# Attention with all products of a pair of key blocks with V in one group on TensorE, and the band factors of both blocks together

## What is computed

```python
q = x @ Wq.T + bq + ocr_bias          # k, v alike; 16 heads of 32 features
scores = jnp.einsum('bhsd,bhtd->bhst', q, k) / math.sqrt(HEAD_DIM)
scores = scores + _band_mask(S, scores.dtype)     # 0.1 where |i - j| <= 2
attn = jax.nn.softmax(scores, axis=-1)
out = jnp.einsum('bhst,bhtd->bhsd', attn, v)
return out @ Wo.T + bo
```

## Time and profile before

| | us |
|---|---|
| median of three runs (lowest to highest) | 4579.53 (4577.45 to 4581.79) |
| the profiled execution, its own time | 4576.01 |
| its span in the trace | 4574.1 |
| TensorE busy in the span (97%) | 4436.7 |
| VectorE busy (74%) | 3378.5 |
| ScalarE busy (53%) | 2446.5 |
| GpSimd busy (62%) | 2828.9 |

### The profile page before, as it was taken

The page is one execution under the profiler, slowest core; times in us unless marked ns, Lnnn a source line. Parts: engine busy times, 40 slices in busy tenths (PEclk is TensorE's granted clock), DMA queues, the critical chain, the costliest instruction groups (busy, mean ns, idle before and its releaser), DMA issues. The chain is left out here.

```text
span 4574.1 us, 62800 instructions
## 1 busy us (share of the span) xinstructions
PE 4436.7 (97%) x22928; PEld 2504.6 (55%) x22928; DVE 3378.5 (74%) x5663; ACT 2446.5 (53%) x4652; POOL 2828.9 (62%) x927
## 2 busy tenths in 40 slices
PE   7999989999999999999999999999999999977999
PEld 6888845454445444444445454444454444525777
DVE  5444467888888888788787888888888788735776
ACT  2222216666666666666666666666666666651121
POOL 2111017778878787787877778878787787870000
PEclk9999969999999999999999999999999999988999
DMA  7666545555565656565656555565656565445452
GB/s 253 206 212 205 197 120 118 129 124 131 125 140 117 140 113 145 110 144 121 142 118 132 128 124 131 125 140 117 140 113 144 112 144 117 104 89 199 147 178 108
DMA packets 287700, 640.71 MB, mean 140 GB/s; under 512 B 40641, under 2 KB 107201, under 8 KB 249538
## 3 DMA queue, kind: packets, MB, share of 16 engines
q0 software_dynamic: 36864, 268.45, 29.3%
q1 hardware_dynamic: 250562, 368.66, 27.0%
HBM read 211.82 MB, written 156.24 MB: 80 GB/s over the span
## 5 line engine op out<-in xcount | busy, mean ns | idle before, releaser
L702 DVE TENSOR_REDUCE part_max<-ps_m 128x1 f32<-128x512 f32 x4096 | 2548.9, 683 | 654.0 <-PE ps_m L598 650.5
L772 POOL TENSOR_TENSOR pair<-p_sb 128x2048 f32<-128x2048 f32 x512 | 2348.4, 4587 | 665.5 <-ACT p_sb L690 301.9
L690 ACT ACTIVATE p_sb<-ps_s 128x512 f32<-128x512 f32 x4096 | 2114.8, 602 | 1130.3 <-PE ps_s L618 1129.8
L618 PE MATMUL ps_s<-q_st,k_st 97*128 97x512 f32 x4096 | 1732.4, 425 | 17.1 <-ACT p_sb L690 17.1
L598 PE MATMUL ps_m<-k_st,q_st 96*128 96x512 f32 x4096 | 1646.0, 405 | 42.0 <-POOL k_st L765 20.1
L618 PEld LDWEIGHTS ps_s<-q_st,k_st 97*128 97x128 f32 x4096 | 774.0, 189 | 1031.4 <-ACT p_sb L690 619.3
L632 PE MATMUL ps_o<-p_sb,v_sb 128*32 128x512 f32 x8192 | 1092.4, 605 | 0.2 <-DVE p_sb L729 0.2
L598 PEld LDWEIGHTS ps_m<-k_st,q_st 96*128 96x128 f32 x4096 | 785.7, 192 | 230.6 <-DVE part_max L702 76.3
L632 PEld LDWEIGHTS ps_o<-p_sb,v_sb 128*32 128x32 f32 x8192 | 161.3, 108 | 345.2 <-ACT p_sb L690 289.3
L166 POOL TENSOR_TENSOR xb<-xin,bo_row 128x2048 f32<-128x2048 f32 x16 | 75.3, 4706 | 424.7 <-DMA xin<-in_x 414.0
L642 PE MATMUL ps_d<-pair,ones 128*32 128x512 f32 x2048 | 267.5, 594 | 9.9 <-DMA pair<-pair 9.9
(11 more groups left out here) (94 smaller groups left out, 2678.4 us busy)
## 6 DMA issues: line engine op xcount, KB each, us to landing
pair<-pair POOLq DMA_DIRECT2D x256, 1024.0 KB, 7.3
q_st<-q_hi_d SPq DMA_DIRECT2D x128, 256.0 KB, 4.2
k_st<-k_hi_d SPq DMA_DIRECT2D x128, 256.0 KB, 5.5
xin<-in_x SPq DMA_DIRECT2D x16, 1024.0 KB, 8.2
xb_d<-xb SPq DMA_DIRECT2D x16, 1024.0 KB, 5.2
q_hi_d<-s_hi SPq DMA_DIRECT2D x64, 256.0 KB, 2.0
q_lo_d<-s_lo SPq DMA_DIRECT2D x64, 256.0 KB, 2.3
k_hi_d<-s_hi SPq DMA_DIRECT2D x64, 256.0 KB, 2.3
```

What stands on the lines that cost most here:

```text
L618: nc.tensor.matmul(ps_s[:, (HG * s + h) % RING_S, :], k_st[0:ROWS + 1, unit // QC % 2, kt // TT, h, kt % TT * P:(kt % TT + 1) * P], q_st[0 ...
L690: nc.scalar.activation(p_sb[:, s % SLOTS, h, :], ps_s[:, (HG * s + h) % RING_S, :], ACT.Exp, scale=SCALE).then_inc(p_ready, 1)
L702: nc.vector.tensor_reduce(part_max[:, unit % 2, col, n:n + 1], ps_m[:, seq % RING_M, :], AX.X, ALU.max).then_inc(max_taken, 1)
L772: nc.gpsimd.tensor_tensor(pair[:, m % PAIR_RING], p_sb[:, s % SLOTS], p_sb[:, (s + 1) % SLOTS], ALU.add).then_inc(paired, 1)
```

## The change

- TensorE: `weigh` of a macro's two steps and, if one is due, `add_keys` now stand together. This burst comes at odd s, after heads 0 and 1 of step s and before head 2, and has `weigh(s - 3)`, `weigh(s - 2)` and at s mod 4 = 1 `add_keys`. `add_keys` keeps its step and comes half a step earlier in it. Even steps have no product with V.
- VectorE: the two bands of macro m (steps 2m and 2m+1) stand after head 1's reduction of step 2m+2, not in front of the first one of that step.
- ScalarE: `copy_o` moves from the start of kt = 2 to the middle of kt = 1, `copy_sum` from the start of kt = 7 to the middle of kt = 5, `o_high` from the start of kt = 14 to the start of kt = 15.
- No instruction is added or removed. SyncE and GpSimd keep their programs.

```diff
--- before.py
+++ after.py
@@ -648,15 +649,20 @@
             for j in range(HG * LEAD):
                 ahead(1, j)
-            for s in range(ST + SUM_LAG - 3):
-                if s < ST:
-                    for h in range(HG):
-                        score(s, h)
-                        ahead(*max_at(s, h))
-                if 2 <= s < ST + 2:
+            def burst(s):
+                if 3 <= s < ST + 3:
+                    weigh(s - 3)
                     weigh(s - 2)
                 if s >= SUM_LAG and s % 4 == SUM_LAG % 4:
                     add_keys((s - SUM_LAG) // 4)
+
+            for s in range(ST + SUM_LAG - 3):
+                for h in range(HG):
+                    if s % 2 == 1 and h == HG // 2:
+                        burst(s)
+                    if s < ST:
+                        score(s, h)
+                        ahead(*max_at(s, h))
 
         @block.scalar
         def _(act):
@@ -676,16 +682,17 @@
             for s in range(ST):
                 unit, kt = s // KT, s % KT
-                if kt == 2 and unit > 0:
-                    copy_o(unit - 1)
-                if kt == 7 and unit > 0:
-                    copy_sum(unit - 1)
-                if kt == 14 and unit > 0:
+                if kt == 15 and unit > 0:
                     o_high(unit - 1)
                 if s >= SLOTS:
                     act.wait_ge(pv_done, s - SLOTS + 1)
                     act.wait_ge(paired, (s - SLOTS) // 2 + 1)
                 for h in range(HG):
+                    if h == HG // 2 and unit > 0:
+                        if kt == 1:
+                            copy_o(unit - 1)
+                        if kt == 5:
+                            copy_sum(unit - 1)
                     act.wait_ge(scored, HG * s + h + 1)
@@ -739,14 +746,15 @@
             for m in range(NM):
-                if m > 0:
-                    spread_band(2 * m - 1)
                 for s in (2 * m, 2 * m + 1):
                     for h in range(HG):
                         ahead(*max_at(s, h))
-                spread_band(2 * m)
+                        if h == 1 and s % 2 == 0 and s > 0:
+                            spread_band(s - 2)
+                            spread_band(s - 1)
                 if m % PAIRS == 4 and m > PAIRS:
                     invert(m // PAIRS - 1)
+            spread_band(2 * NM - 2)
             spread_band(2 * NM - 1)
             invert(NU - 1)
```

## The result

The changed kernel takes 4781.71 us (median of 4 runs, 4780.26 to 4785.44) against 4578.49 for the kernel before on the same chip. The ratio is 1.044, with a 95% interval of 1.042 to 1.046: slower by 203 us. The forecast was 4773. The profiled execution took 4780.26, its span 4778.5.

The account below looks back on a forecast made before the run. TensorE was taken to set the pace, with VectorE second but slower inside a step. Terms +51 + 163 - 55 + 25 + 10 = +194 us on 4576.0 gave 4770, as median 4773; range 4700 to 4870.

Parts of the forecast that it names:

- Part 1, one burst for two: TensorE, plain macros: one change per macro saves 0.31 us, the last maximum's wait loses 0.41; +51 us in all.
- wait of the last maximum: Run of eight on TensorE: maximum 7 needs reduction 4, ready at 4.02 against 3.61, so waits 0.41 us.
- Part 2, the bands: VectorE, behind a run's fourth reduction: two wide bands delay TensorE by 1.22 us; +163 us, earlier costs of 55 go.
- Collisions with GpSimd: Bands against GpSimd's sums: close to none in the new place, 27 us gone; rival of collisions in runs: 5067, 5%.
- Part 3, the row of maxima: Unit's end: score 0 of the next unit waits 0.6 us for `shift`, +25 us; `turn` and `rows` on VectorE, +10.
- The clock: Rival: TensorE's clock falls in banded macros, 3.2 us each, +400 us, near 5170; chance 3%.
- a stall like the 0.60 of the earlier trace left the clock alone: TensorE's clock: the kernel before held 2.4 GHz over such stalls, said against the rival of a falling clock.
- sign of being wrong: Profile after: bursts 5.8 apart, paired bands longer than 1.31, or a clock under 1.00 in the middle of the span.
- The sum: Whole kernel: +51 + 163 - 55 + 25 + 10 = +194 us on 4576.0, giving 4770, as median 4773.
- chance of slower: Whole kernel: slower 88%, faster 9%, within 0.2% 3%.
- What is moved and costs nothing: ScalarE's `copy_o`, `copy_sum`, `o_high` and later pair sums: moves absorbed by slack, no cost; `copy_sum` 13 us at worst.

Follow-up runs that it names:

- pair without bands: The kernel before and the changed kernel, each with the band factors left out: 4516.41 us and 4570.93 us.
- VectorE's part alone: The kernel before with only VectorE's new order of bands: 4751.44 us; the same with `o_high` moved to kt = 15: 4637.30 us.
- half reductions: The changed kernel with row maxima taken over half of each block's columns: 4477.26 us; the kernel before with the same: 4516.23 us.
- bands_alone: The kernel before with both steps' bands behind the second reduction of an even step, `o_high` left at kt = 14: 4751.44 us.
- late_sums: The changed kernel with bands behind a run's eighth reduction, a maximum first and last in each run, key sums two steps later: 4546.93 us.

## Why the prediction was right, step by step

- *Part 1, one burst for two.* The mechanism held. The saving of 0.31 is seen bare where reductions are quick (5.8 against 6.1). The wait of the last maximum was forecast as a weight load 3.91 into the run (4.02 less the exposed 0.11), and it stands at 3.91. Bursts were forecast 6.2 apart and are 6.20. The difference of the two was less exact: I took 6.10 for two steps from a single one of 3.05, their mean is 6.13, and so a macro loses 0.06 to 0.07 and not 0.10. That makes some 33 us, not 51.
- *Part 2, the bands.* 1.22 per pair in full: runs of 5.6 us and bursts 7.4 and 8.3 apart, as forecast. Per kernel the bands' worth is 211 us after and 63 before. With 42 us of the 211 due to the clock, 169 are left against the 163 of the sum, and 63 stand against 55.
- *Collisions with GpSimd.* Forecast as close to none, and in the changed kernel there is none between 1000 and 4000 us (no band over 706 ns). By the rule of the Trainium skill quoted there (SBUF — State Buffer, section Who interferes with whom) they were to be feared. The changed kernel's last unit, with a band of 4.0 us beside a pair sum, agrees with the rule; before that the two don't meet in time.
- *Part 3, the row of maxima.* The second term that was too large. I had +25 for waits on `shift` and +10 for `turn` and `rows`. The pair without bands shows some 18 us for both, by the distances above; of its 54.5 us, 54.5 - 33 - 18 = about 4 have no place in this account. Scores do wait for `shift` now:

```profile
PEld ps_s L619 <- DMA q_st<-shift: 26.6, 35, 1.8
PE ps_s L619 <- DMA q_st<-shift: 10.8, 23, 1.4
```

  but of each idle stretch of the weight loads up to 0.84 is there in any case behind products with V, and VectorE's extra work partly replaces the 0.26 that a transposition costs TensorE otherwise (without bands the plain macro near the unit's end is 6.32 long, not 6.19).
- *The clock.* It was a rival with 3%, as a fall in all banded macros at 3.2 us each. What happened lies between: it falls behind 22 of 422 macros, for one burst, 1.3 to 1.7 us each, 42 us in all. The statement that a stall like the 0.60 of the earlier trace rows left the clock alone was right; that it would also be so at 1.5 us wasn't. This is the one sign of being wrong that came: the mean granted clock between 1000 and 4000 us is 0.99 and not 1.00.
- *The sum.* +194 forecast, +203 measured: 33 + 18 + 4 + 169 + 42 - 63 = 203. The 169 and the 4 are what is left of measured totals and not readings of their own. It came out 9 us from the forecast because misses of opposite sign met, about -18 in part 1 and -17 in part 3 against +42 in the clock. That is luck. The range and the chance of slower didn't need it: without the clock's 42 us the time would be about 4740, still inside 4700 to 4870.
- *What is moved and costs nothing.* True for the change as it stands. VectorE's part alone shows how close it may have been: in the kernel with one group of products with V per step, later bands with `o_high` left at kt = 14 cost 114 us more than with it at kt = 15. I had described that move as harmless, not as needed. The changed kernel with `o_high` at kt = 14 wasn't run.

## What to carry to other kernels

Before two groups of work are merged to save a change of mode, count what the group in between feeds: a ring of three banks covers a run of four when the reader needs 0.60 us and the writer 0.47, not one of eight, and the saved 0.31 us came back as a wait of 0.41. In such a run everything that is put ahead of the reader's decisive item (here the first five reductions) is on the path in full, and the same work beside the burst is free, until the next consumer in the chain is late (band, pair sum, merge, sums). Where a run must stay long, let it begin with the item that the slower engine reads: that order alone gave 121 us.

## What the runs showed of the hardware

- TensorE's granted clock fell to its lower level for about one burst behind waits of 1.53 us (0.63 over the 4.6 us from 2044.0), 22 times in 3000 us, 14 of them behind a single such wait with plain macros ahead of it; and once in a kernel whose longest such waits were 1.3 us. At the margin a small change of a wait was worth 42 us.
- A band that met a GpSimd instruction took up to 4.0 us in the changed kernel for a work of 0.7 (4.9 with half reductions), with 8 elements 1.76 for 0.16.
- The landing of the 8 KB row `shift` took 5.7 us (median) in the kernel before and 1.8 when issued a step earlier in the unit, with the same bytes. What it meets is GpSimd's merging DMA of 1024 KB. In the kernel before all 56 rows between 1000 and 4000 us were issued while one was under way, and landed at about the same time as it (median difference 0.0 us); with the early transposition none of 52 was. `bands_alone` has both kinds in one trace: 26 rows issued beside a merging DMA landed in 5.3 to 6.5 us, the other 27 in 1.8 to 2.2. In `late_sums` the row has its old place again, only one of 56 meets more than the last us of such a DMA, and it lands in 1.8 (median).
